# A selective scan beside routed experts: the first quarter of the scan moved into the attention stage, expert rows scatter-added, and a product moved from GpSimd to VectorE

## The chip, the cores and the metric

One core of a Trainium2 chip runs the whole kernel in one launch, in float32. Its engines are TensorE (PE in the rows, with PEld for its weight loads), VectorE (DVE), ScalarE (ACT), GpSimd (POOL) and SyncE (SP), which issues most DMAs. The metric is the device time of one execution in microseconds, and lower is better. Each engine works through its own instructions in order and waits on semaphores that the others raise, so the place of an instruction in its engine's order matters as much as its duration.

## The reference, cut to what matters

`x` is 4 sequences (batches) of 512 tokens with 512 features, `ctx` is 4 x 512 x 256. Four blocks follow one another, each with a residual addition:

```python
x = x + attention(layernorm(x), ctx)      # energy = (ctx Wq + bq)(ctx Wk + bk)^T, softmax, mixes feature rows
x = x + moe16(layernorm(x))               # 16 experts of 192, top 2 per token, weights from a softmax
x = x + mamba(ctx, layernorm(x))          # selective scan over ctx, gated by silu(layernorm(x))
x = x + ffn2(layernorm(x))                # 2 of 8 experts of 2048, chosen once for all tokens

# mamba, for one batch: 512 channels, 16 states per channel, 512 time steps
xin = in_proj(ctx); u = silu(conv4(xin) + conv_b)
dt_low, Bm, Cm = split(x_proj(u)); dt = softplus(dt_proj(dt_low) + dt_b)
state = state * exp(dt * A) + (dt * u) * Bm      # the recurrence over time
y = sum_n(state * Cm) + D * u;  out = y * silu(z)
```

What the scan needs comes from `ctx` alone. Only its gate `z` needs the result of the first two blocks. In moe16 a token's two expert outputs are weighted and added to the token's row `x1`, which gives `x2`.

## The kernel before, in words

The work runs in five stages.

1. **The sequence stage**, a loop over the 4 batches (`sequence_pe`, `sequence_act`, `sequence_dve`, `sequence_transfers`; `rstd_of` on GpSimd). Per batch: queries and keys, four energy tiles (L1460), softmax (`row_max`, `normalize`), transposes (L1437), the mixing products (L1474), the sum with x (L1148), a layernorm, its transposes, the router scores (L1494). Between these lie the scan's inputs: `in_proj` (L1430) for the next batch, the convolution (`convolve`, L1108 and L1114), silu (L856), `x_proj` (L1480), `dt_proj` (L1484), and the softplus of `dt`, whose exp and ln are on ScalarE (L866, L871) and whose five passes over 128x2048 are on VectorE (`softplus`, L1131 to L1140). The step sizes `DT` and `DTU` of all batches stay in SBUF; u, the rows of B and C, x1 and the normalised rows go to DRAM.
2. **The routing stage**: VectorE ranks the tokens by expert and makes one-hot tables `row_hot` and `tile_hot` (L1229 to L1238), and TensorE turns them into the slot list `slot_tok` with 32 products (L1516). There are 48 slot tiles of 128 rows.
3. **The recurrence stage** holds the scan and the 16 experts together. The scan is cut into 128 units, 32 a batch. A unit is one block of 128 channels with two states: ScalarE makes the decay (`decay`, two exps, L892), GpSimd `dt*u*B` (`dbu`, L728), VectorE scans (L1247) and multiplies with C (`read_out`, L1256), TensorE adds the two products to y (`add_states`, L1534); after each four units ScalarE takes y out of its bank (`take_y`). The expert path of a tile is: gather rows of xn by an indirect DMA from GpSimd (`gather`, L742), transpose (L1554), gate and up products (`up`, L1561), a copy to SBUF and tanh on ScalarE, gate times up on GpSimd (`gate_by_up`, L734), `finish_h` on VectorE (L1262), transpose, the down product (`down`, L1579), a scaled copy to `YT` and a plain store of it to `expert_rows`. The interleaving is written out by hand: 8 units ahead, then a fixed share of the remaining ones in each tile:

```python
AHEAD = 8
ALL = B * UB
cuts = [AHEAD + (ALL - AHEAD) * j // SLOT_TILES for j in range(SLOT_TILES + 1)]
...
for j in range(SLOT_TILES):          # VectorE
    for i, u in enumerate(units(j)):
        scan(*bu(u))
        if i == 1 and j + 1 < SLOT_TILES:
            finish_h(0, j + 1)
        read_out(*bu(u))
```

   so a tile has 2.5 units. In a tile TensorE does `turn_h(j)`, `up(j+1)`, some units, `turn_x(j+2)`, more units, `down(j)`.
4. **The combine stage**, per batch: GpSimd gathers each token's two expert rows (`gather_y`, eight indirect DMAs a batch), VectorE adds them with their weights to x1 (`add_first`, `add_second`), takes the statistics, gates y and adds (`combine`); ScalarE and TensorE normalise, transpose and make the logits of the last block (`silu_z`, `turn_gated`, L1000 to L1008). At its end the two experts are known.
5. **The last feed-forward stage**, bound to TensorE by its three-term products (L1664, L1675).

## Time and profile before

| | |
|---|---|
| median of three runs | 1596.02 us (1595.16 to 1596.70) |
| profiled execution, first to last instruction | 1594.7 us |
| its own time beside that span | not reported apart from the three runs; their median is 1.3 us above the span |
| TensorE, matmul busy | 1391.5 us (87%) |
| VectorE busy | 936.9 us (59%) |
| GpSimd busy | 784.0 us (49%) |
| ScalarE busy | 709.8 us (45%) |
| chain that ended last | TensorE 58%, VectorE 22%, issue 10% |

The span has five stages with different limits, so the shares over the whole say little. In the page's 40 slices VectorE is at 9 tenths only in slices 8 to 18, which is the recurrence stage; TensorE is at 9 in the last 18 slices, the last feed-forward. Between them both are partly idle. A row of a stage has to be read against that stage's own length.

### The profile page before, as it was taken

The page shows a single profiled execution, that of the slowest core. Times are in us where ns is not written, and L with a number is a line of the kernel's source. Part 1 is how long each engine was busy: PE and PEld are TensorE (multiplying, and loading weights), DVE is VectorE, ACT ScalarE, POOL GpSimd, SP SyncE. Part 2 cuts the span into 40 slices and gives each one's busy share as a digit, 9 for nine tenths or more (in the row PEclk, how much of TensorE's full clock was granted, in tenths as well). Part 3 has the DMA queues.
Part 4 walks back from the last instruction along what each step waited for, and adds up shares of the span by engine and source line. Part 5 has one row for each costly group of instructions (what it writes and reads, how often), then busy time and mean ns, then how long its engine had stood idle before and what let it go on. Part 6 is the DMA issues. An engine that isn't in the chain of part 4 may idle for free.

```text
span 1594.7 us, 18873 instructions
## 1 busy us (share of the span) xinstructions
PE 1391.5 (87%) x6080; PEld 1030.4 (65%) x6080; DVE 936.9 (59%) x1186; ACT 709.8 (45%) x1303; POOL 784.0 (49%) x607
## 2 busy tenths in 40 slices
PE   6988983588899989897166999999999999999998
PEld 3535532566666656664166787878787887878786
DVE  2677767999999999998683224241414224241413
ACT  4445433266766776665143333333333333333332
POOL 0000000788888988885631445444544545444442
PEclk9898895699999999999555999999999999999999
DMA  3202214477977987863655900010000100010000
GB/s 105 108 26 81 107 53 165 158 240 257 315 257 234 319 269 264 281 198 125 218 198 203 364 14 0 0 66 1 14 0 13 52 13 0 0 53 0 0 0 26
DMA packets 78202, 191.29 MB, mean 120 GB/s; under 512 B 10856, under 2 KB 15752, under 8 KB 77120
## 3 DMA queue, kind: packets, MB, share of 16 engines
q1 hardware_dynamic: 64832, 157.03, 29.3%
q0 software_dynamic: 6400, 20.98, 4.1%
q10 hardware_dynamic: 6912, 12.59, 2.2%
q8 instruction: 28, 0.46, 0.1%
q14 instruction: 30, 0.25, 0.0%
HBM read 152.55 MB, written 38.01 MB: 119 GB/s over the span
## 4 chain that ended last, share of the span: by engine, by line
PE 58%; DVE 22%; issue 10%; ACT 4%; POOL 3%; DMA 3%; ACTq 0%; SPq 0%; DVEq 0%; POOLq 0%
PE decay L1675 22%; PE bank L1664 21%; DVE decay L1247 11%; DVE S L1256 4%; PE bank L1474 2%; PE decay L1430 2%; PE bank L1437 1%; DVE XH L1114 1%; PE bank L1494 1%; PE bank L1534 1%; PE decay L1484 1%; PE bank L1619 1%; POOL Y L767 1%; PE bank L1561 1%; PE decay L1480 1%
## 5 line engine op out<-in xcount | busy, mean ns | idle before, releaser
L1387 DVE CAST HFH<-HF 128x512 fp32r<-128x512 f32 x128 | 59.0, 461 | 496.7 <-ACT HF L1045 496.7
L815 POOL TENSOR_TENSOR W2L<-W2R,W2H 128x512 fp32r<-128x512 f32 x128 | 172.5, 1347 | 348.2 <-ACT W2H L1040 348.2
L728 POOL TENSOR_TENSOR S<-DTU,Bb 128x1024 f32<-128x1024 f32 x128 | 304.7, 2401 | 25.1 <-DVE row_hot L1229 21.7
L1247 DVE TENSOR_TENSOR_SCAN decay<-decay,S 128x1024 f32<-128x1024 f32 x128 | 292.9, 2288 | 0.5 <-ACT decay L892 0.5
L1664 PE MATMUL bank<-XSH,W1H 128*128 128x512 f32 x512 | 202.9, 396 | 4.2 <-POOL W1L L811 4.2
L1675 PE MATMUL decay<-W2H,HFH 128*128 128x512 f32 x512 | 200.4, 391 | 5.3 <-DVE HFL L1389 5.3
L1664 PE MATMUL bank<-XSH,W1L 128*128 128x512 f32 x512 | 203.0, 396 | 0.0
L1664 PE MATMUL bank<-XSL,W1H 128*128 128x512 f32 x512 | 202.3, 395 | 0.0
L1675 PE MATMUL decay<-W2L,HFH 128*128 128x512 f32 x512 | 199.9, 390 | 0.0
L1675 PE MATMUL decay<-W2H,HFL 128*128 128x512 f32 x512 | 199.7, 390 | 0.0
L811 POOL TENSOR_TENSOR W1L<-W1R,W1H 128x512 fp32r<-128x512 f32 x128 | 171.1, 1337 | 49.6 <-ACT W1H L1031 49.6
L1040 ACT CAST W2H<-W2R 128x512 fp32r x128 | 79.4, 620 | 230.0 <-PE decay L1675 229.7
L1045 ACT ACTIVATE HF<-bank,b1T 128x512 f32<-128x512 f32 x128 | 88.3, 690 | 195.4 <-PE bank L1664 195.3
L892 ACT ACTIVATE decay<-DT,negA 128x511 f32<-128x511 f32 x256 | 166.3, 683 | 0.0
L1534 PE MATMUL bank<-ident,S 128*128 128x128 f32 x1024 | 136.9, 284 | 32.3 <-ACT U L933 16.3
L1256 DVE TENSOR_TENSOR S<-decay,Cb 128x1024 f32<-128x1024 f32 x128 | 156.1, 1219 | 4.2
L1534 PEld LDWEIGHTS bank<-ident,S 128*128 128x128 f32 x1024 | 122.8, 148 | 54.5 <-issue 28.3
L1561 PE MATMUL bank<-WGU,XGT 128*128 128x384 f32 x384 | 133.3, 491 | 0.7 <-ACT XGT L900 0.7
L695 POOL TENSOR_TENSOR rstd<-vare,minus_half 128x4 f32<-128x4 f32 x8 | 8.1, 1011 | 227.4 <-DVE vare L1072 227.4
L1675 PEld LDWEIGHTS decay<-W2H,HFH 128*128 128x128 f32 x512 | 96.1, 188 | 30.2 <-issue 8.8
L1664 PEld LDWEIGHTS bank<-XSH,W1H 128*128 128x128 f32 x512 | 96.6, 189 | 27.1 <-POOL W1L L811 5.7
L1664 PEld LDWEIGHTS bank<-XSH,W1L 128*128 128x128 f32 x512 | 96.5, 188 | 23.1
(212 smaller groups left out, 2102.3 us busy)
## 6 DMA issues: line engine op xcount, KB each, us to landing
WGU<-in_L_ffn_gate_w SPq DMA_DIRECT2D x48, 384.0 KB, 3.8
WGU<-in_L_ffn_up_w SPq DMA_DIRECT2D x48, 384.0 KB, 5.1
WD<-in_L_ffn_down_w SPq DMA_DIRECT2D x48, 384.0 KB, 4.9
Bb<-bc_rows SPq DMA_DIRECT2D x32, 512.0 KB, 7.9
Cb<-bc_rows SPq DMA_DIRECT2D x32, 512.0 KB, 9.7
expert_rows<-YT ACTq DMA_DIRECT2D x48, 256.0 KB, 4.2
W1R<-in_L_ffn_w SPq DMA_DIRECT2D x6, 1024.0 KB, 13.9
W2R<-in_L_ffn_w SPq DMA_DIRECT2D x6, 1024.0 KB, 14.1
```

The lines of the kernel that those rows point to most:

```text
L728: pool.tensor_tensor(S[u % NP][:], DTU[:, ds(b, 1), c, :].to_broadcast([P, PAIR, L]), Bb[j][:], ALU.mult).then_inc(dbu_ready, 1)
L811: pool.tensor_tensor(W1L[f % 2][:], W1R[:, ds(e, 1), :, f * P:(f + 1) * P].rearrange("p e k f -> p (e k) f"), W1H[f % 2][:].bitcast(F32), ...
L815: pool.tensor_tensor(W2L[f % 2][:], W2R[:, ds(e, 1), f, :].rearrange("p e d -> p (e d)"), W2H[f % 2][:].bitcast(F32), ALU.subtract).then_i ...
L892: ins = act.activation(DA[u % 2][:, i, 1:], DT[:, ds(b, 1), c, 1:].rearrange("p b l -> p (b l)"), ACT.Exp, scale=negA[:, c, j * PAIR + i:j ...
L1040: act.copy(W2H[f % 2][:], W2R[:, ds(e, 1), f, :].rearrange("p e d -> p (e d)")).then_inc(w2h_ready, 1)
L1045: act.activation(HF[f % 2][:], PS[4 + f % 2][:], ACT.Gelu_apprx_tanh, bias=b1T[:, ds(e, 1), f:f + 1].rearrange("p e f -> p (e f)")).then_i ...
L1247: dve.tensor_tensor_scan(flat, flat, S[u % NP][:].rearrange("p i l -> p (i l)"), 0.0, ALU.mult, ALU.add).then_inc(scan_done, 1)
L1256: dve.tensor_tensor(S[u % NP][:], DA[u % 2][:], Cb[j][:], ALU.mult).then_inc(hc_ready, 1)
L1534: ins = pe.matmul(YS[:, t * P:(t + 1) * P], st[:, i, t * P:(t + 1) * P], ident[:], start=(i0 + i + t == 0), stop=False, is_transpose=True, ...
L1561: ins = pe.matmul(UP[:, 0:2 * F].rearrange("p (g f) -> p g f", g=2), XGT[n % 2][:, k, :], WGU[n % 2][:, :, k, :], start=(k == 0), stop=(k ...
L1664: ins = pe.matmul(PS[4 + f % 2][:], w[f % 2][:, k, :], v[half][:, k, :], start=(k == 0 and i == 0), stop=(k == K - 1 and i == 2))
L1675: ins = pe.matmul(PS[t][:], u_[f % 2][:, t * P:(t + 1) * P], w[f % 2][:], start=(f == 0 and i == 0), stop=(f == FT - 1 and i == 2))
```

## The change

The scan's first batch (32 units) moves into the sequence stage, eight units a round, one round beside the attention of each batch and the projections of the next. The projections and step sizes of batch 0 are now made before the first round. The loops over batches become written-out rounds. 80 units remain for the 48 tiles, eight before them and eight behind them. The PSUM banks 5 to 7 go round in one fixed list of jobs, each waiting until the job three before it has been read. Three of the softplus passes move to GpSimd (`step_sizes`), both layernorm applications to ScalarE (`norm_x`, `norm_x1`). The expert outputs are weighted in the copy to `YT` and added straight into the rows of x1 in DRAM by an indirect DMA with an addition; the gathers and additions of the combine stage go. The slot table carries weights as well as tokens. Gate times up moves from GpSimd to VectorE.

```diff
-        AHEAD = 8
-        cuts = [AHEAD + (ALL - AHEAD) * j // SLOT_TILES for j in range(SLOT_TILES + 1)]
+        EARLY = UB
+        ROUND = EARLY // B
+        AHEAD = EARLY + 2 * HP
+        cuts = [AHEAD + (ALL - AHEAD - TAIL) * j // SLOT_TILES for j in range(SLOT_TILES + 1)] + [ALL]
...
 # GpSimd
+            def step_sizes(b):
+                dt, dtu, rl = DT[:, b], DTU[:, b], XP[:, :, TAPS - 1:]
+                pool.wait_ge(nd_ready, b + 1)
+                pool.tensor_tensor(rl, rl, ZZ[:], ALU.subtract).then_inc(size_made, 1)
+                pool.wait_ge(ln_ready, b + 1)
+                pool.tensor_tensor(dt, rl, dt, ALU.add).then_inc(size_made, 1)
+                pool.tensor_tensor(dtu, dt, dtu, ALU.mult).then_inc(dt_ready, 1)
...
+            for b in range(B):
+                n = b * ROUND
+                products(n + 3, n + ROUND)
+                scale_and_shift1(2 * b + 2)
+                products(n + ROUND, n + ROUND + 2)
+                if b + 1 < B:
+                    scale_and_shift1(2 * b + 3)
+                    step_sizes(b + 1)
+                products(n + ROUND + 2, n + ROUND + 3)
...
+            def add_rows(j):
+                pool.wait_ge(yt_ready, j + 2)
+                if j:
+                    pool.wait_ge(yt_added, j * DMA)
+                pool.indirect_dma_start(out=x2_rows, out_offset=bass.IndirectOffsetOnAxis(ap=slot_dst[:, j:j + 1], axis=0),
+                                        in_=YT[j % 2][:], in_offset=None, compute_op=ALU.add).then_inc(yt_added, DMA)
...
             for j in range(SLOT_TILES):
                 for u in units(j):
                     dbu(*bu(u))
-                gate_by_up(j)
+                if j >= 2:
+                    add_rows(j - 2)
                 if j + 2 < SLOT_TILES:
                     gather(0, j + 2)
...
 # ScalarE, one round
+                exp_e(b, 0); exp_e(b, 1); decays(n + 1, n + 2)
+                take_turned("v", b, 0, XNT); take_turned("v", b, 1, XNT)
+                exp_e(b, 2); exp_e(b, 3); decays(n + 2, n + 3)
...
+                silu_u(b + 1); decays(n + 6, n + 7)
+                take_qk(b + 1); take_xd(b + 1); decays(n + 7, n + 8)
+                norm_x1(b); size_abs(b + 1)
+                for t in range(T): take_turned("n", b, t, XNT)
+                size_exp(b + 1); take_scores(b); size_ln(b + 1); norm_x(b + 1)
+                decays(n + 8, n + 9)
...
 # VectorE, one round
+                row_max(b, 0); row_max(b, 1); unit(n)
+                normalize(b, 0); row_max(b, 2); normalize(b, 1); row_max(b, 3); unit(n + 1)
+                normalize(b, 2); normalize(b, 3); unit(n + 2)
+                convolve(b + 1, (0, 1)); unit(n + 3); unit(n + 4); convolve(b + 1, (2, 3)); unit(n + 5)
+                add_x(b, 0); add_x(b, 1); unit(n + 6); add_x(b, 2); add_x(b, 3); statistics_x1(b); unit(n + 7)
+                positive_part(b + 1); statistics_x(b + 1); correction(b + 1)
...
 # VectorE, routing and tiles
+                for t in range(NT):
+                    dve.tensor_scalar(tile_hot[:, k, t, 0, :], iota_j[:], jf[:, k, t:t + 1], tokid[:, t:t + 1], ALU.is_equal, ALU.mult)
+                    ins = dve.tensor_scalar(tile_hot[:, k, t, 1, :], iota_j[:], jf[:, k, t:t + 1], rwt[:, k, t:t + 1], ALU.is_equal, ALU.mult)
...
+                    last = i == len(units(j)) - 1 and j + 1 < SLOT_TILES
+                    if last:
+                        gate_by_up(j + 1)
                     scan(*bu(u))
-                    if i == 1 and j + 1 < SLOT_TILES:
+                    if last:
                         finish_h(0, j + 1)
                     read_out(*bu(u))
...
 # TensorE, one round (the last without the steps of b + 1)
+                energy(b, 0); energy(b, 1); turn_xn(b, 0); turn_xn(b, 1); sums(n - 1, n)
+                energy(b, 2); energy(b, 3); sums(n, n + 1); turn_xn(b, 2); turn_xn(b, 3)
+                turn_ctx(b + 1); in_proj(b + 1, (0, 1)); sums(n + 1, n + 2); in_proj(b + 1, (2, 3))
+                turn_p(b, 0); turn_p(b, 1); sums(n + 2, n + 3); turn_p(b, 2); turn_p(b, 3); sums(n + 3, n + 4)
+                mix(b, 0); mix(b, 1); sums(n + 4, n + 5); mix(b, 2); mix(b, 3); sums(n + 5, n + 6)
+                queries_keys(b + 1); x_proj(b + 1); sums(n + 6, n + 7); dt_proj(b + 1)
+                turn_xn1(b, t) for the four t; score(b)
...
 # VectorE, combine: add_first and add_second are gone
+            for u in units(SLOT_TILES):
+                scan(*bu(u))
+                read_out(*bu(u))
+            statistics_x2(0)
+            statistics_x2(1)
```

The diff is cut: calls that stand on lines of their own in the code are put together here.

## Rows read from the trace of the kernel before

**Rows 1.** Windows by stage: length, busy of PE PEld DVE ACT POOL, clock, DMA, GB/s.

```profile
0.00:262.20 262.20, 214.94 (x696) 115.00 (x696) 164.69 (x285) 118.03 (x174) 10.84 (x19) 0.88 0.22 77
262.20:294.50 32.30, 2.04 (x4) 1.17 (x4) 29.07 (x101) 2.81 (x7) 10.40 (x8) 0.50 0.80 292
294.50:752.30 457.80, 407.36 (x2038) 285.92 (x2038) 447.28 (x306) 298.94 (x665) 379.68 (x271) 0.96 0.74 242
752.30:862.20 109.90, 55.04 (x268) 51.35 (x268) 71.42 (x161) 35.80 (x55) 44.50 (x54) 0.57 0.59 201
862.20:1594.70 732.50, 712.13 (x3074) 576.97 (x3074) 224.49 (x339) 254.18 (x402) 338.59 (x256) 0.99 0.11 40
```

**Rows 2.** Timeline of the sequence stage: start us, us, engine line operation.

```profile
21.30 7.13 PE L1430 MATMUL decay<-ctxT,inT 128*128 128x512 f32 x16 [0.40 <-ACT gate2T L823]
...
34.39 0.69 DVE L1088 TENSOR_REDUCE nmax<-bank 128x1 f32<-128x512 f32 x1 [7.99 <-PE bank L1460]
```

**Rows 3.** Windows, one batch of the sequence stage, from one first row maximum to the next.

```profile
34.39:93.01 58.62, 53.29 (x161) 27.60 (x160) 41.30 (x71) 26.94 (x39) 2.02 (x2) 0.85 0.20 73
```

**Rows 4.** Groups by line and shape in one batch: busy us, mean ns, idle before.

```profile
L1474 PE MATMUL bank<-ATT,XNT 128*128 128x512 f32 x32 | 14.3, 599 | 1.4 <-DVE X1A L1148 0.7 <-ACT ATT L838 0.7
L1114 DVE SCALAR_TENSOR_TENSOR XH<-XP,convW,XH 128x512 f32<-128x512 f32 x12 | 8.2, 747 | 0.1
L1133 DVE SCALAR_TENSOR_TENSOR ND<-XH,ZZ 128x2048 f32<-128x2048 f32 x1 | 2.3, 2293 | 0.0
```

**Rows 5.** Timeline around the end of the sequence stage.

```profile
255.24 1.91 ACT L871 ACTIVATE ZZ<-XH 128x2048 f32<-128x2048 f32 x1 [2.22 <-DVE ND L1133]
...
262.17 1.31 DVE L1172 MAX8 M<-SC 128x8 f32<-128x16 f32 x16
```

**Rows 6.** Windows, the router scores of two batches, at two granted clocks.

```profile
129.50:136.50 7.00, 7.00 (x33) 7.00 (x34) 4.04 (x12) 5.45 (x6) 1.01 (x1) 0.50 0.01 3
246.10:250.20 4.10, 4.08 (x32) 3.98 (x32) 0.00 (x0) 4.07 (x6) 0.00 (x0) 0.90 0.00 0
```

**Rows 7.** Timeline: the slot tables, and a small tensor_scalar of the combine stage.

```profile
284.63 3.96 DVE L1233 TENSOR_TENSOR tile_hot<-iota_j,jf 128x768 f32<-128x768 f32 x2
...
288.63 5.99 DVE L1238 TENSOR_TENSOR tile_hot<-tile_hot,tokid 128x768 f32<-128x768 f32 x2
...
294.67 13.89 PE L1516 MATMUL bank<-tile_hot,row_hot 128*128 128x48 f32 x64 [24.91 <-DVE tile_hot L1238]
...
861.07 0.36 DVE L1362 TENSOR_SCALAR loh<-iota_e,lidf 128x8 f32<-128x8 f32 x2
```

**Rows 8.** Groups by shape in 300 us of the recurrence stage (400 to 700).

```profile
L728 POOL TENSOR_TENSOR S<-DTU,Bb 128x1024 f32<-128x1024 f32 x85 | 200.6, 2380 | 0.8
L1247 DVE TENSOR_TENSOR_SCAN decay<-decay,S 128x1024 f32<-128x1024 f32 x85 | 194.5, 2289 | 0.5 <-ACT decay L892 0.5
L1256 DVE TENSOR_TENSOR S<-decay,Cb 128x1024 f32<-128x1024 f32 x85 | 103.6, 1219 | 2.6
L1534 PE MATMUL bank<-ident,S 128*128 128x128 f32 x680 | 90.0, 282 | 19.3 <-ACT U L933 11.8 <-ACT DTU L935 7.4
L1554 PE MATMUL bank<-ident,XG 128*128 128x128 f32 x135 | 23.5, 296 | 10.3 <-DMA XG<-xn_rows,gcol 5.6 <-ACT HT L910 4.6
L1262 DVE SCALAR_TENSOR_TENSOR GU<-bank,GU 128x192 f32<-128x192 f32 x34 | 11.6, 342 | 2.0 <-POOL GU L734 2.0
```

**Rows 9.** DMA issues of the recurrence stage: count, size, median us to landing.

```profile
expert_rows<-YT ACTq DMA_DIRECT2D x48, 256.0 KB, 4.2
...
XG<-xn_rows,gcol POOLq DMA_INDIRECT x48, 6.2
```

**Rows 10.** Timeline of the combine stage.

```profile
764.77 2.74 DVE L1299 SCALAR_TENSOR_TENSOR X<-Y,rwt,X 128x512 f32<-128x512 f32 x4 [12.44 <-DMA Y<-expert_rows,pcol]
...
846.92 2.93 ACT L1000 ACTIVATE ZN<-X,shift,rstd 128x512 f32<-128x512 f32 x4
...
858.90 0.19 ACT L1008 COPY logits<-bank 128x32 f32<-128x32 f32 x1 [2.63 <-PE bank L1619]
```

1076 lines of the change are left out of this document (623 added, 453 removed).

## The prediction

> **What bounds the kernel now.** I read the windows by stage first, because the limits differ [rows 1]. The sequence stage (0 to 262.2) has TensorE busy 82%, VectorE 63%, GpSimd 4%. The recurrence stage (294.5 to 752.3) has VectorE busy 447.3 of 457.8 us: it is the limit there, and TensorE with 407.4 us (89%) is close behind. The combine stage (109.9 us) has no engine over 65%. The last stage, 732.5 us, is TensorE's and isn't touched: I leave it as it is. So the reader is to see a full VectorE in one stage, room on VectorE in another, and a TensorE that is nearly full in both. Moving scan units helps by what VectorE gets rid of until TensorE binds; where they go, they cost what the tighter order of the rounds makes of them.
>
> I sum against the profiled span, 1594.7 us. The median of the three runs is 1.3 us above it and I add that at the end.
>
> **Sequence stage, the period of a round.** Now a batch takes 58.6 us, with TensorE busy 53.3 and VectorE 41.3 [rows 3]. In the new round VectorE loses two layernorm applications and three passes of 2.3 us [rows 4] (some 11 us) and gains eight units. A unit is 2.29 + 1.22 = 3.5 us [rows 8], so 28 us: about 58 to 60 us of work. TensorE gains eight times 90.0/85 = 1.06 us, the additions of U (1.6) and the transposes of ctx (2): about 65 us as this row counts it. Neither sum is the period, for the orders of the engines chain. I followed one round from the first scan (time 0), with durations of 0.7 for a 128x512 operation on VectorE, 0.55 for a copy and 1.4 for a decay on ScalarE, 3.6 for one mixing product (14.3/4, rows 4) and 3.6 for x_proj or a pair of in_proj ([rows 2]: four channels in 7.1):
> - three units with the softmax between them end at 14.6; the first half of the convolution (8.2/2 for its additions plus 1) waits for two in_proj copies at 15.2 and ends at 20; two units, 27; the second half, 32; sixth unit, 35.7;
> - x_add needs two mixing products, done in time; seventh unit 40.5; x_add and statistics 45;
> - the eighth unit waits for its decay, which stands on ScalarE behind `take_xd`: TensorE can begin x_proj only at 45.3, since the third mixing bank is freed at 41 and the keys come first. x_proj 48.9, copy 49.5, decay 50.9, unit 54.4: a stall of 5.9 us;
> - positive part 57.4 with the fourth dt product waiting for a bank; the four transposed copies of the normalised x1 end at 60.3; exp 62.3; correction (1.2 + 2.3) 65.9;
> - scores on TensorE until 65 to 68, and ScalarE takes them before its ln: ln, a table load of 1.3, four normalisations 2.9, a decay 1.4. The next first scan comes at 75 to 78.
>
> So a round is 76.5 us. Its last third holds some 10 us in which VectorE has only two row maxima. GpSimd's three passes of 128x2048 (estimate 2 x 2.38 = 4.8 each [rows 8]) end 4.6 us after the first scan, and its third unit product at 7.1 is due at 11.1: hidden; on less cover (a round 4 us shorter there) they would be the wait.
>
> First scan of round 0: in_proj starts at about 21.9 instead of 21.3 [rows 2], convolution in halves to 36, silu, x_proj, dt_proj and positive part to 47.7, exp and correction 54.5, ln and three passes on VectorE (7) 61.4, first product and decay 64. Three periods: 293.5. The last round has no next batch: units and additions to 35.9, statistics, normalisation, transposes, scores to 51: 344.5. Before, the routing began at 262.2 [rows 5]. **+82.3 us.**
>
> At this point the clock matters. The same 32 score products take 7.0 us at a granted clock of 0.50 and 4.1 at 0.90 [rows 6], so the level of 1.2 GHz costs up to 3 us in each round in which TensorE has waited before; the range 75 to 78 holds it. The Trainium skill (TensorE: Matmul & The Clock Gate, What's actually happening) says that idleness brings the half clock and activity releases it; the rounds add idle gaps on TensorE, and by that rule every round would pay the 7 and not the 4, which is the 78 end: three rounds at 78 give +4.5 us, no other outcome.
>
> **Routing.** `tile_hot` was four operations, 3.96 + 5.99 = 9.95 us [rows 7], and is 64 tensor_scalars of 128x48. No row has these; a 128x8 one with a scalar operand has a pitch of 0.18 (0.36 for two). I take 0.20: 12.8 us, **+2.9**; ends 0.08 (the pitch of the 128x16 maxima, 1.31/16, rows 5) and 0.25 give -4.8 and +6. The slot products get 96 columns instead of 48: 64 in 13.9 us at clock 0.50, 0.217 each [rows 7]; with 16 columns they also take 0.217 (7.0/32 [rows 6]), so columns are nearly free: +1, at most 8. Five small operations on the slot sums, 1.2 us. **+2.2.** `spare_row` and the removed `pos` cast: nothing.
>
> **Recurrence stage.** Eight units before the tiles and eight behind are VectorE's, 28 us each. Between them 48 tiles of 1.67 units instead of 2.5. VectorE needs 1.67 x 3.5 = 5.8 plus gate times up (0.35, as its neighbour of the same 192 columns) and finish: 6.3 us. TensorE: 407.4 minus the slot products 13.9 minus 128 x 1.06 leaves 257.8, or 5.37 a tile; with 1.67 units 7.14, of which about 0.2 falls with the additions of U: 6.95. To this its waits: 19.3 us in 85 units for y being taken (0.38 a tile) and 10.3 in 34 tiles for gathered rows (0.30) [rows 8]. That is 7.6 us: **TensorE binds instead of VectorE.** The loop through the copy of gate and up, the product on VectorE, a whole scan, finish, transpose and the next up product is 0.5 + 0.35 + 2.3 + 0.35 + 0.2 + 2.75, 6.5 us, just under it: the product before the last scan stalls VectorE, but not the tile. GpSimd: 1.67 x 2.38 and two indirect DMAs at about 1.3: 6.6, covered. So 28 + 48 x 7.6 + 28 = 420.8 against 457.8: **-37.0 us.**
>
> The new wait is in `add_rows`: the DMA of tile j-2 waits until that of j-3 has landed, and behind it on GpSimd stand the gather of tile j+2 and the unit products; for them wait TensorE's transposes and VectorE's scan. No row shows an adding DMA. A plain store lands in 4.2 us, an indirect gather in 6.2 [rows 9]. I take 7, near the gather; 4.2 is the low end, and twice the gather, 12.4, the high one. Up to 7.6 it costs nothing. The rule in the Trainium skill (DMA: Bandwidth & Descriptors, Two DMAs through the same engine are not ordered) speaks against shortening this: dependent DMAs need the first one's completion, so the chain can't overlap, and the tile can't be shorter than the landing. No run here shows it yet; it is the third rival below.
>
> DMA traffic: the stage moved 242 GB/s at a share of 0.74 [rows 1], so 327 at full share. The tiles carry 48 x 1.7 MB (weights 1.18, rows in and out 0.52) and 20 MB of B, C and u, 102 MB in 365 us, 280 GB/s, 0.86: it fits; if an addition takes its bytes twice, 0.96, and the margin is gone.
>
> **Combine.** Before: VectorE idles 12.4 us for the first gathers [rows 10], and the stage is 109.9 us. Now the loads of x2 run under the last eight units. Statistics 3.2, power and shift 1.4, silu 2.9, last transposes 0.9: 8.6 us; gate, add, statistics, shift 9.7: first normalisation at 18.3. Per batch then 12.0 from normalisation to logits (846.92 to 858.90 [rows 10]) and 2.9 for the next silu before it: 18.3 + 4 x 12.0 + 2 x 2.9 + 0.5 = 72.6, plus 3.3 to the end of the stage: 76. Half the TensorE work at a higher clock would give 66. **-33.9 us.**
>
> **Sum:** 82.3 + 2.9 + 2.2 - 37.0 - 33.9 = +16.5. 1594.7 + 16.5 + 1.3 = **1612.5 us**.
>
> **Rivals.**
> - *The tiles run at TensorE's bare work* (the waits for y and for rows vanish since ScalarE and DMA have more room a tile): 6.95 us, -31 us, **1581**, faster. For it: the engine that caused the order of waits, VectorE, is off the path. Against: those waits came with ScalarE 65% busy in the stage [rows 1], not with a full one. It decides from a tile under 7.19 us (16.5 + 3.2 over 48).
> - *The rounds overlap better than my chain*: with banks and decays in time a round is TensorE's 66 us: -31.5, **1581**. For it: TensorE is the fuller engine. Against: `decays` stand behind `take_xd` and behind the ln in the order.
> - *The adding DMA lands late*: at 9.5 us a tile is 9.5: +91, **1704**; at 8.5 +43, **1656**. Decides from 7.6 us. For it: the read before the write; against: a load of 0.86 is not full.
> - *The change's parts cancel*: either faster case by half, **1596**.
>
> **Numbers.** Forecast with its own spread (1600 to 1630) 0.52; bare tiles 0.15; overlapping rounds 0.11; late additions 0.14; cancelling 0.08. What can be told from no change here is 0.2%, 3.2 us. Faster 0.15 + 0.11 = 0.26; same 0.08; slower 0.66. The range that leaves 2 in 10 out reaches over both faster cases' middle and the mild form of the late one: 1576 to 1650.
>
> **What would show it.** Right: the first slot-table maximum near 345 and first rows of maxima 76 us apart; in the tiles TensorE over 90% and VectorE about 83%; from the last read-out to the last expert choice 76 us. Wrong: a period near 66, a tile under 7.2 us, or a wait of GpSimd on the landing of the added rows in most tiles. The last stage longer or shorter than 732 us would mean that something I left alone was touched.

## The result and the profile after

The kernel after took 1721.0 us (median of four runs, 1707.05 to 1722.28) against 1595.6 of the kernel before: a ratio of 1.077, 95% interval 1.073 to 1.081. The forecast was 1612.5 in a range of 1576 to 1650: the sign was right, the size was not, and the range did not hold it. The profiled execution of the kernel after spans 1720.5 us, the one of before 1594.7, so the stages below add up to the whole difference. Where the runs of one kernel spread by more than 1.5% (x2 and x11 below), only those within that of the quickest are compared.

Windows of the kernel after by stage: length, busy time of PE PEld DVE ACT POOL, granted clock, DMA share, GB/s. They answer to [rows 1]; the recurrence is cut here into the units ahead of the tiles, the tiles, and the units behind them.

```profile
0.00:391.70 391.70, 282.51 (x968) 163.26 (x969) 274.88 (x316) 189.18 (x312) 129.78 (x68) 0.77 0.24 81
391.70:443.50 51.80, 4.38 (x15) 2.35 (x13) 49.68 (x161) 3.40 (x8) 19.11 (x12) 0.53 0.30 119
443.50:472.40 28.90, 21.03 (x116) 18.04 (x116) 28.28 (x22) 11.49 (x25) 10.24 (x7) 0.71 0.40 137
472.40:885.60 413.20, 351.14 (x1582) 228.77 (x1583) 311.60 (x259) 231.49 (x510) 308.39 (x173) 0.94 0.84 238
885.60:915.20 29.60, 15.61 (x62) 11.03 (x60) 24.17 (x16) 10.55 (x23) 12.64 (x6) 0.58 0.46 151
915.20:988.70 73.50, 54.65 (x268) 50.51 (x268) 49.87 (x129) 35.49 (x55) 10.24 (x16) 0.57 0.35 129
988.70:1720.50 731.80, 711.73 (x3074) 576.80 (x3074) 224.35 (x338) 254.17 (x402) 338.51 (x256) 0.99 0.11 40
```

| stage, us | before | after | difference | forecast |
|---|---|---|---|---|
| sequence | 262.2 | 391.7 | +129.5 | +82.3 |
| routing | 32.3 | 51.8 | +19.5 | +2.9 |
| recurrence | 457.8 | 471.7 | +13.9 | -34.8 (with the slot sums) |
| combine | 109.9 | 73.5 | -36.4 | -33.9 |
| last feed-forward | 732.5 | 731.8 | -0.7 | 0 |

So three terms failed and two held. Of the 109 us between forecast and time, 47 are in the sequence stage, 17 in the routing and 49 in the recurrence stage; the combine stage takes 2.5 back.

The forecast's own signs agree with this. The first slot-table maximum comes at 391.7 instead of near 345. In the tiles TensorE is busy 85% and VectorE 75% (351.14 and 311.60 of 413.20 us), where over 90% and about 83% were named for the right case. The sign of the late addition, a wait of GpSimd on the landing of the added rows in most tiles, did not come either: it waits so in 10 of the 48, 34.4 us in all.

**Routing.** The timeline of the kernel after, at the slot tables (start, duration, engine, line, operation). All 64 tensor_scalars have one shape; while GpSimd's eight unit products run (413.14 to 431.56), each takes 2.33 to 2.38, and from the moment these end, 0.29 at a pitch of 0.215.

```profile
412.97 0.30 DVE L1447 TENSOR_SCALAR CbT<-iota_j,jf,tokid 128x48 f32<-128x48 f32 x1
413.19 2.33 DVE L1449 TENSOR_SCALAR CbT<-iota_j,jf,rwt 128x48 f32<-128x48 f32 x1
415.44 2.38 DVE L1447 TENSOR_SCALAR CbT<-iota_j,jf,tokid 128x48 f32<-128x48 f32 x1
...
429.22 2.38 DVE L1447 TENSOR_SCALAR CbT<-iota_j,jf,tokid 128x48 f32<-128x48 f32 x1
431.52 0.29 DVE L1449 TENSOR_SCALAR CbT<-iota_j,jf,rwt 128x48 f32<-128x48 f32 x1
431.73 0.29 DVE L1447 TENSOR_SCALAR CbT<-iota_j,jf,tokid 128x48 f32<-128x48 f32 x1
...
413.14 18.42 POOL L774 TENSOR_TENSOR S<-DTU,Bb 128x1024 f32<-128x1024 f32 x8 [20.71 <-DVE row_hot L1442]
```

**Rounds.** Two rounds of the kernel after, from first scan to first scan. The third takes 88.0. Forecast: 76.5, with TensorE busy 65, and busy it is for 65.5 and 67.7.

```profile
70.09:156.80 86.71, 65.46 (x228) 36.62 (x228) 67.27 (x78) 46.13 (x77) 30.87 (x15) 0.80 0.16 56
156.80:246.25 89.45, 67.65 (x240) 39.12 (x240) 70.51 (x78) 46.10 (x77) 34.91 (x16) 0.79 0.29 101
```

VectorE's groups by shape in the second of them: busy us, mean ns | idle before. In [rows 4] the same shapes took 747 ns (convolution) and 2293 (correction).

```profile
L1322 DVE TENSOR_TENSOR_SCAN decay<-decay,S 128x1024 f32<-128x1024 f32 x8 | 18.3, 2293 | 11.0 <-ACT decay L996 11.0
L1275 DVE SCALAR_TENSOR_TENSOR DTU<-XP,convW,DTU 128x512 f32<-128x512 f32 x12 | 12.6, 1093 | 0.2
L1331 DVE TENSOR_TENSOR S<-decay,Cb 128x1024 f32<-128x1024 f32 x8 | 9.8, 1224 | 0.3
L1264 DVE TENSOR_SCALAR X1A<-X1A,rinv 128x512 f32<-128x512 f32 x4 | 4.8, 1212 | 0.1
L1297 DVE SCALAR_TENSOR_TENSOR ZZ<-DT,ZZ 128x2048 f32<-128x2048 f32 x1 | 4.3, 4318 | 0.0
L1289 DVE TENSOR_SCALAR XP<-bank,dtB 128x512 f32<-128x512 f32 x4 | 2.8, 744 | 1.6 <-PE bank L1658 1.6
```

The reader is to see which rows grew. The scan, the read-out and the positive part have an operand in PSUM (`decay`, `bank`) and kept their durations; the convolution, the normalisation and the correction have all their operands in SBUF and grew. Among those that read one tensor from SBUF, the statistics (BATCH_NORM_STATS2, 0.68 us) did not. The convolution grows in all three rounds (1.09 us each); the correction only in this one, and takes 2.29 us in the other two. The waits for ScalarE's decay (11.0) were in the forecast's chain in part: 5.9 for the eighth unit, and the rest as the wait for the next first decay.

**Tiles.** The starts of ScalarE's copy of gate and up, one a tile, give 47 tile lengths. The median is 7.7 us; the forecast had 7.6 for each. But six tiles take 12.2 to 14.7, 83 us together, and the mean is 8.4. The timeline of the tile that takes 14.7:

```profile
584.57 0.99 POOL L827 DMA_INDIRECT XG<-xn_rows,slot_tok  x1 [0.31 <-issue]
...
588.51 0.47 ACT L1099 COPY GU<-bank 128x384 f32<-128x384 f32 x1
...
592.98 1.60 POOL L836 DMA_INDIRECT x_rows<-YT,slot_dst  x1 [5.02 <-DMA x_rows<-YT,slot_dst]
594.31 1.12 PE L1789 MATMUL bank<-ident,XG 128*128 128x128 f32 x4 [5.15 <-DMA XG<-xn_rows,slot_tok]
594.88 0.99 POOL L827 DMA_INDIRECT XG<-xn_rows,slot_tok  x1 [0.30 <-issue]
...
603.19 0.48 ACT L1099 COPY GU<-bank 128x384 f32<-128x384 f32 x1 [1.63 <-PE bank L1796]
603.70 0.43 DVE L1457 TENSOR_TENSOR GU<-GU 128x192 f32<-128x192 f32 x1 [10.08 <-ACT GU L1099]
```

GpSimd waits 5 us for the landing of the last addition, and the next gather and the unit products stand behind it. But the rows for which TensorE waits 5 us are not those: they are of the gather issued at 584.57, before that wait, and it was itself 9.7 us on the way. VectorE then stands 10 us in front of the gate product, behind which its scans stand.

Five of the six long tiles begin like this one: in the tile before them an addition and, 1.9 us behind it, a gather are issued, and both take 8.3 to 10.8 us to land. In these stretches the DMA engines are full. SyncE has put loads of B and C (512 KB each) and of u beside the weights of the experts there. Windows over two of the five, from the issue of the late addition to the landing of the gather, and over the sixth tile (DMA share and GB/s are the last two numbers):

```profile
582.70:594.30 11.60, 6.08 (x26) 3.43 (x25) 10.88 (x10) 6.11 (x14) 6.26 (x4) 0.95 1.04 302
764.50:777.20 12.70, 6.14 (x26) 3.82 (x26) 9.06 (x9) 5.94 (x13) 7.63 (x6) 0.88 1.05 303
852.60:866.90 14.30, 9.35 (x38) 5.84 (x36) 12.85 (x6) 3.68 (x9) 7.91 (x5) 0.76 0.24 49
```

Of the 96 gathers and additions of this kernel, 41 share no moment with a load of B, C or u; they land after 5.9 us in the median and 7.5 at most. 43 share one with two or more such loads, and their median is 7.7; all 20 that take over 8 us are among them. The sixth long tile has nothing of this. It holds one of the two gate products that GpSimd shut out in these tiles (the other, 4.26 us long, comes right behind it):

```profile
853.15 5.83 DVE L1457 TENSOR_TENSOR GU<-GU 128x192 f32<-128x192 f32 x1 [3.65 <-ACT GU L1099]
```

### The profile page after: what moved, and what is told of

It is laid out like the page before. It is cut to its first block, busy times and chain, and to the rows that moved or that the text cites. A ratio compares the mean times of both kernels' runs of the same rounds, so it can differ in the third digit from the quotient of the medians.

```text
span 1720.5 us, 18682 instructions
## 1 busy us (share of the span) xinstructions
PE 1441.0 (84%) x6080; PEld 1050.8 (61%) x6080; DVE 962.8 (56%) x1234; ACT 735.8 (43%) x1334; POOL 828.9 (48%) x536
## 3 DMA queue, kind: packets, MB, share of 16 engines
q0 software_dynamic: 10752, 25.17, 6.8%
## 4 chain that ended last, share of the span: by engine, by line
PE 49%; DMA 8%; DVE 8%; issue 5%; POOL 4%; ACT 3%; SPq 0%; ACTq 0%; DVEq 0%; POOLq 0%
PE decay L1916 20%; PE bank L1905 20%; DMA XG<-xn_rows,slot_tok 5%; PE bank L1796 2%; DMA x_rows<-YT,slot_dst 2%; DVE decay L1322 2%; PE bank L1814 2%; PE bank L1702 2%; POOL S L774 2%; POOL x_rows L836 2%; DVE S L1331 1%; DVE CbT L1447 1%; PE bank L1860 1%; DVE CbT L1449 1%; ACT decay L996 1%
## 5 line engine op out<-in xcount | busy, mean ns | idle before, releaser
L1702 PE MATMUL bank<-ident,S 128*128 128x128 f32 x1024 | 152.4, 300 | 44.8 <-DVE S L1331 38.9
L1702 PEld LDWEIGHTS bank<-ident,S 128*128 128x128 f32 x1024 | 133.7, 156 | 78.9 <-DVE S L1331 45.2
L836 POOL DMA_INDIRECT x_rows<-YT,slot_dst x48 | 76.8, 1599 | 87.4 <-ACT YT L1112 50.4
L1331 DVE TENSOR_TENSOR S<-decay,Cb 128x1024 f32<-128x1024 f32 x92 | 112.2, 1219 | 3.2
## 6 DMA issues: line engine op xcount, KB each, us to landing
W1R<-in_L_ffn_w SPq DMA_DIRECT2D x6, 1024.0 KB, 13.9
W2R<-in_L_ffn_w SPq DMA_DIRECT2D x6, 1024.0 KB, 14.7
```

The source lines that it names most:

```text
L836: pool.indirect_dma_start(out=x2_rows, out_offset=bass.IndirectOffsetOnAxis(ap=slot_dst[:, j:j + 1], axis=0), in_=YT[j % 2][:], in_offset= ...
L1331: dve.tensor_tensor(state(b, u)[:], DA[u % 2][:], Cb[rows(b, j)][:], ALU.mult).then_inc(hc_ready, 1)
L1702: ins = pe.matmul(YS[:, t * P:(t + 1) * P], st[:, i, t * P:(t + 1) * P], ident[:], start=(i0 + i + t == 0), stop=False, is_transpose=True, ...
```

## The experiments

Two theories were tested against the rivals "slow by themselves", "hidden anyway" and "the DMA engines are full". (A) VectorE and GpSimd shut each other out when both read SBUF. (B) The order of gather, addition and gate product in GpSimd's and VectorE's queues makes the long tiles. Stage lengths of all kernels, each of its profiled execution. The tiles go here from the first scan of the first tile to the first scan behind the last one, 403.5 us in the kernel after (the 413.2 of the windows above begins some 6 us earlier and ends 3.5 later); combine ends with the choice of the two experts.

| kernel | sequence | routing | 8 ahead | tiles | behind | combine |
|---|---|---|---|---|---|---|
| before | 262.2 | 32.3 | 28.4 | 429.4 | none | 108.4 |
| after | 391.7 | 51.8 | 35.1 | 403.5 | 33.1 | 71.9 |
| x1 products behind `tile_hot` | 389.2 | 38.6 | 35.9 | 399.8 | 33.2 | 71.8 |
| x2 gather first | 390.6 | 52.8 | 34.8 | 566.0 | 32.3 | 71.5 |
| x3 no addition | 385.0 | 51.8 | 34.5 | 389.4 | 31.9 | 71.3 |
| x4 none early, gate on GpSimd | 310.1 | 38.6 | 32.8 | 448.4 | 32.3 | 71.2 |
| x5 two targets | 390.3 | 37.7 | 35.7 | 385.2 | 31.9 | 71.2 |
| x6 decays earlier | 383.2 | 37.7 | 36.1 | 401.8 | 31.9 | 71.2 |
| x7 sizes on VectorE | 386.5 | 37.6 | 36.2 | 398.2 | 32.2 | 71.5 |
| x8 gate on GpSimd | 388.5 | 38.6 | 32.9 | 420.8 | 32.0 | 71.7 |
| x9 short products | 357.5 | 38.6 | 35.7 | 399.5 | 33.3 | 71.7 |
| x10 sixteen early | 358.5 | 38.6 | 31.0 | 421.4 | 31.5 | 71.3 |
| x11 none early, gate on VectorE | 314.6 | 38.6 | 32.8 | 522.3 | 30.4 | 71.2 |
| x12 before, products behind `tile_hot` | 258.6 | 28.8 | 33.0 | 429.2 | none | 108.7 |
| x13 gather first, gate on GpSimd | 388.6 | 52.7 | 30.7 | 391.2 | 33.0 | 72.0 |
| x14 rounds mended | 382.7 | 37.7 | 36.4 | 393.9 | 32.5 | 71.5 |
| x15 before, four behind | 262.7 | 32.4 | 28.4 | 412.8 | 14.5 | 101.4 |
| x16 before, eight behind | 262.6 | 32.4 | 28.4 | 415.5 | 30.6 | 101.0 |
| x17 x15 and x12 | 260.8 | 28.7 | 32.9 | 420.2 | 15.9 | 100.6 |
| x18 after, all mended | 382.9 | 37.7 | 31.6 | 397.1 | 31.4 | 71.2 |

Each row is one execution, so small differences in it mean nothing. Six kernels have the same code in the sequence stage (after, x1, x2, x3, x8, x13), and it takes 385.0 to 391.7 us there; six have the same code in the tiles (after, x1, x6, x7, x9, x14), which take 393.9 to 403.5.

### The shut-out in the routing

```diff
-            pool.wait_ge(hot_ready, 1)      # x1; x12 the same on the kernel before, with 1 + TOP
+            pool.wait_ge(hot_ready, 2)
```

> GpSimd makes the eight products ahead of the tiles only when tile_hot is complete (it waited for row_hot alone). Theory: VectorE and GpSimd shut each other out of a shared path to the memory, so the eight 128x48 tensor_scalars that take 2.33 to 2.38 us each while GpSimd's products run fall to about 0.29 with a pitch of 0.215; tile_hot takes 64 x 0.215 = 13.8 us instead of 30.4, the first scan behind it waits 2.4 for its product, so the stage of the routing is 51.8 - 16.6 + 2.6 = 38 us and the kernel 1707. Rival: the first eight are slow by themselves (the start of a run of such instructions, or CbT's place); then they stay at 2.3 and the kernel is 1721 + 2.4 = 1723.

1705.7 us, ratio to before 1.068 (1.064 to 1.073). The routing fell from 51.8 to 38.6, as the theory had it: all 64 operations now take 0.30. The rival falls.

> The kernel before (1595.4 us), with GpSimd's first products behind tile_hot instead of behind row_hot. Theory of the shared path: its four operations on tile_hot, which took 9.95 us while a product ran, take about 0.9 each (768 columns at the 1.08 ns a column of the 4096 of row_hot), 3.5 in all, and the first scan then waits 2.4 for its product: 1591. Rival: they take 10 us by themselves, and the wait adds 2.4: 1598.

The kernel before had the same shut-out, and [rows 7] shows it. The timeline of x12:

```profile
281.10 1.82 DVE L1233 TENSOR_TENSOR tile_hot<-iota_j,jf 128x768 f32<-128x768 f32 x2
282.95 1.83 DVE L1238 TENSOR_TENSOR tile_hot<-tile_hot,tokid 128x768 f32<-128x768 f32 x2
...
287.37 2.30 DVE L1247 TENSOR_TENSOR_SCAN decay<-decay,S 128x1024 f32<-128x1024 f32 x1 [2.59 <-POOL S L728]
```

3.65 us instead of 9.95, and 2.59 given back in the wait for the first product; the units ahead take 4.6 longer. The kernel is not told from unchanged (ratio 0.9998, 0.9987 to 1.0009): the theory's durations are right and its 1591 us is not.

### The shut-out in the rounds

```diff
+                w = slice(0, L // 8 if n < EARLY else L)
-                pool.tensor_tensor(state(b, u)[:], DTU[:, b:b + 1, c, :]..., Bb[rows(b, j)][:], ALU.mult)
+                pool.tensor_tensor(state(b, u)[:, :, w], DTU[:, b:b + 1, c, w]..., Bb[rows(b, j)][:, :, w], ALU.mult)
```

> On the kernel in which the products wait for tile_hot (1705.7 us, sequence 389.2, rounds of 87.5, 86.6 and 88.9). GpSimd's products of the 32 units in the rounds cover only the first 64 of the 512 columns (left out: the rest of the rows of batch 0, which keep a zero; four more memsets at the start). All waits and all work of the other engines stay. Theory: the products shut VectorE out: its normalisations go from 0.74 to 1.3 us back to 0.49, the additions of the convolution from 1.09 to 0.75, the correction from 4.3 to 2.3, together 9 to 10 us a round; 7 of them shorten the round: sequence 365, kernel 1682. Rival: VectorE's longer operations only fill time in which it would wait for TensorE and ScalarE; the round stays within 1.5 us: 1701 to 1710.

1678.4 us, against 1705.7 for the kernel that it changes; sequence -31.7 (forecast of the theory: -24). The rounds are 78.3, 77.7 and 78.4 us. VectorE's groups in the second round of x9:

```profile
L1278 DVE SCALAR_TENSOR_TENSOR DTU<-XP,convW,DTU 128x512 f32<-128x512 f32 x12 | 8.6, 755 | 0.2
L1292 DVE TENSOR_SCALAR XP<-bank,dtB 128x512 f32<-128x512 f32 x4 | 2.8, 746 | 1.6 <-PE bank L1661 1.6
L1300 DVE SCALAR_TENSOR_TENSOR ZZ<-DT,ZZ 128x2048 f32<-128x2048 f32 x1 | 2.4, 2426 | 0.0
```

Against x1 the rounds are 9.2, 8.9 and 10.5 us shorter, 9.5 in the mean, and VectorE is busy 9.2, 9.8 and 6.9 us less in them. With the shut-out by unit products gone the round is within 2 us of the 76.5 of the forecast. VectorE waits for decays 10.2 us in this round, against 11.0 in the kernel after, so that wait isn't the difference. Nor is it that the shorter products come earlier: in the rounds of x1 no scan waits for a product.

```diff
-                    step_sizes(b + 1)                 # GpSimd, x7
+                    first_step_sizes(b + 1)           # VectorE, behind correction(b + 1): the same three passes
```

> On the kernel in which the products wait for tile_hot (1705.7 us). The three passes of 128x2048 that make the step sizes of batches 1 to 3 are VectorE's again (2.3 us each, 6.9 a round, behind the correction) and not GpSimd's (4.2 to 4.6 each, 13 a round). Theory: GpSimd's passes shut VectorE out for about as long as VectorE would need for them (normalisations 1.29 us instead of 0.49, additions of the convolution 1.0 instead of 0.75): VectorE's others become short again and the round changes by -2 to +2 us: kernel 1700 to 1712. Rival: GpSimd's passes were hidden and free, the round becomes 5 to 7 us longer three times: 1721 to 1727.

1697.9 us, ratio 1.065 (1.062 to 1.069), not told from x1's 1.068 (1.064 to 1.073). VectorE works 7.7, 8.0 and 5.4 us more in a round and the round stays (88.8, 88.4, 86.3 beside 87.5, 86.6, 88.9). The result is that of the theory, but only a part of its reason holds: the convolution stays at 1.09 us, so it was the unit products that made it long, while the four normalisations of the second and third round fall to 0.49 us each, from 0.74 and 1.13. Most of the passes fits into time in which VectorE stood: its idle time in a round fell from 19.8, 18.0 and 21.7 to 13.4, 11.8 and 13.7 us.

```diff
-                take_qk(b + 1); take_xd(b + 1); decays(n + 7, n + 8)
+                decays(n + 7, n + 8); take_qk(b + 1); take_xd(b + 1)
...
-                size_exp(b + 1); take_scores(b); size_ln(b + 1); norm_x(b + 1); decays(n + 8, n + 9)
+                size_exp(b + 1); decays(n + 8, n + 9); take_scores(b); size_ln(b + 1); norm_x(b + 1)
```

> On the kernel in which the products wait for tile_hot (1705.7 us, sequence 389.2). On ScalarE the decay of the eighth unit of a round stands ahead of the copies of queries, keys and x_proj, and the decay of the next round's first unit ahead of the scores, the ln and the normalisation. Theory: the two stalls of VectorE in each round (5.9 and 5 to 5.9 us) come from that order; the first goes, of the second half stays since the products need the step sizes: three rounds each 5 us shorter, sequence 374, kernel 1691. Rival: what VectorE waits for next (the fourth dt product, the energies of the next batch) ends no earlier; sequence within 4 us of 389, kernel 1702 to 1710.

1699.9 us, ratio 1.067 (1.063 to 1.070), by itself not told from x1. The sequence is 6.0 shorter in the profiled execution, between the theory's 15 and the rival's 4, and it is 382.7 to 383.2 in all three kernels with this edit (x6, x14, x18), below the 385.0 to 391.7 of those without. The waits for decays are gone from the rounds, and the three together are 11.0 us shorter (81.1, 85.3, 85.6); the last round, 60.3 instead of 55.3, gives 5 back.

### The price of the sequence stage's new order

```diff
-        EARLY = UB
+        EARLY = 0         # x4; with x1's wait and gate_by_up on GpSimd behind the unit products (x11: on VectorE)
```

> No scan unit stands in the sequence stage (all 128 behind the routing, eight ahead of the tiles and eight behind), GpSimd makes the product of gate and up as in the kernel before, and the products wait for tile_hot as in the first run of this call; the adding of rows, the new routing and the new combine stage stay. Theory: the loss is in the rounds, and what the tiles had to gain by fewer units was not there. Sequence 262 to 275, routing 36, recurrence 28 + 48 x 8.4 (2.33 units of 3.5 and 0.2 as in the kernel before) + 28 = 459, combine 73.5, last stage 731.8: 1568, faster than both kernels. Rival 1: the adding DMA holds a tile at 8.6 whatever VectorE does: recurrence 469, 1578. Rival 2: the sequence stage is slow by its new order of banks and copies, not by the units: sequence 300 or more, 1600 or more.

1674.7 us, not 1568, and slower than before by 5%. Rival 2 came: the sequence stage takes 310.1 with no unit in it. The timeline of x4 at its first row maxima, for [rows 2]:

```profile
66.52 0.68 DVE L1241 TENSOR_REDUCE nmax<-bank 128x1 f32<-128x512 f32 x1
...
125.77 0.68 DVE L1241 TENSOR_REDUCE nmax<-bank 128x1 f32<-128x512 f32 x1
...
191.49 0.68 DVE L1241 TENSOR_REDUCE nmax<-bank 128x1 f32<-128x512 f32 x1
```

The first softmax starts at 66.5 instead of 34.4, since the whole input path of batch 0 stands before it: +32.1. The periods are 59.3, 65.7 and then 68.0 instead of 58.6, and the last batch gets a little back: the other 15.8. The units come on top: 389.2 - 310.1 = 79 us for 32.

But about half of the miss of 107 us is in the recurrence stage, 513.5 us where the theory had 459. A version of the kernel before can be set beside it: x16 (below) has the same 8 units ahead, 112 in the tiles and 8 behind, the gate product on GpSimd too, and stores the expert rows. Windows over the tiles of x4 and then of x16:

```profile
381.50:829.90 448.40, 380.36 (x1852) 260.20 (x1850) 393.73 (x272) 278.69 (x613) 409.88 (x252) 0.96 0.84 239
323.40:738.90 415.50, 375.65 (x1854) 259.32 (x1854) 394.46 (x272) 275.13 (x614) 351.07 (x253) 0.97 0.79 258
```

TensorE and VectorE do the same work, GpSimd 59 us more (it issues the additions), and the tiles take 33 us more. The combine stage is 30 shorter (71.2 and 101.0). So the adding path pays in the tiles about what it saves in the combine stage. The two kernels differ in the tiles in small things as well (the place of `finish_h`, the order of the loads), so the 33 us are not shown to be the additions' alone.

```diff
-        EARLY = UB
+        EARLY = 16        # x10: four units a round, tile_hot in the place of three states
```

> Sixteen units in the sequence stage, four a round, instead of 32 (1705.7 us) or none (1674.7); 2.0 units to a tile; the gate product on VectorE, tile_hot in the place of three states. Theory: a unit costs 2.5 us in a round (389.2 - 310.1 over 32), so sequence 350; a tile of 2.0 units has 7.7 us of VectorE and 8 of TensorE and takes 8.5: tiles 408; routing 38, ahead and behind 68, combine 71, last stage 734: 1669 and 3 more: 1672. Rival: TensorE, whose units are moved and not removed, holds the tile at what 1.58 units take (8.3): tiles 400, 1664. Other rival: the late rows of the gathers grow with the density of the stage: tiles 424, 1688.

1690.1 us, near the third guess. Sixteen units cost 48 us in the sequence stage, the next sixteen 31. What the tiles gain by them depends on the engine of the gate product. With it on GpSimd, 32 early units shorten the tiles from 448 (x4) to 421 (x8), for 79 us in the rounds. With it on VectorE the tiles go from 522 (x11, below) to 421 (x10) to 400 (x1): the first sixteen units pay there, the next sixteen don't. None of these kernels is faster than the 1674.7 us with no early unit and the gate product on GpSimd.

### Gather, addition and gate product in the tiles

```diff
-                if j >= 2: add_rows(j - 2)
-                if j + 2 < SLOT_TILES: gather(0, j + 2)
+                if j + 2 < SLOT_TILES: gather(0, j + 2)
+                if j >= 2: add_rows(j - 2)
```

> In GpSimd's order of a tile the gather of tile j+2 stands ahead of the addition of tile j-2 instead of behind it. Theory: the gather is late because it waits in line behind the addition (its 1.6 us of issue, and its wait for yt_ready and for the last landing); TensorE's 40.5 us of waits for gathered rows mostly go, half of it is given back to the next wait: tile stage 413.2 - 20 = 393, kernel 1700. Rival: the rows are late because the DMA engines are full (share 0.84), whatever the order of issue: the waits move, stage within 4 us of 413, kernel 1717 to 1725.

1816.8 us in the one run of four that can be compared: slower by 96 where I had expected 20 faster. The others took 1852.5 to 1884.1, and the profiled execution is the longest of them, so its rows show what happens and not how much of it happens in 1816.8 us. Groups of x2 in its tiles:

```profile
L1457 DVE TENSOR_TENSOR GU<-GU 128x192 f32<-128x192 f32 x47 | 191.2, 4068 | 97.3 <-ACT GU L1099 97.3
L836 POOL DMA_INDIRECT x_rows<-YT,slot_dst x47 | 75.0, 1595 | 253.9 <-ACT YT L1112 253.9
```

The gate product, 0.35 us of work on two operands in SBUF, took 4.07 on average (0.58 in the kernel after): 46 of the 48 met a unit product of GpSimd, 31 of them two in a row, and stood until these were through. It makes a ring: the gate product late, the down product late, YT late, so GpSimd waits 5.4 us for YT and starts its unit products just when the next gate product is due. The next runs test this.

```diff
                 for u in units(j): dbu(*bu(u))
+                gate_by_up(j)                         # GpSimd, x8; gone from VectorE
```

> On the kernel in which the products wait for tile_hot (1705.7 us, tiles 399.8). The product of gate and up of a tile is GpSimd's again, behind the unit products. Theory: VectorE, which stands 94 us in the stage before this product while ScalarE's copy of gate and up isn't there, scans ahead instead; GpSimd has 3.8 + 1.6 + 1.0 + 0.6 = 7.0 us a tile and stays under 8.3: tiles 399.8 - 12 = 388, kernel 1694. Rival: the product comes later behind GpSimd's wait for the landing of the added rows, and the up and down products with it: tiles 410, kernel 1716.

1719.1 us (x1: 1705.7); tiles +21. With the old order the rival was right: the gate product stands behind GpSimd's waits, and VectorE waits some 120 us for it in the tiles.

x11 is x4 with the gate product left on VectorE, x13 the kernel after with the edits of x2 and x8.

> No unit in the sequence stage, as in the run of 1674.7 us, but the product of gate and up is VectorE's. Theory: GpSimd was full in the tiles there (2.33 products of 2.44, 1.6 to issue the addition, 1.0 for the gather, 0.6 for the gate product: 8.9 us with its waits): without the gate product it has 8.3 and VectorE 2.33 x 3.5 + 0.7 = 8.9: tiles 448.4 - 18 = 430, kernel 1657. Rival: VectorE is the limit at 8.9 and stands for ScalarE's copy beside it: tiles 448 or more, 1675.

1746.0 us (median of three runs, ratio 1.095, 1.089 to 1.101): tiles 522 where the theory had 430. Gate products of up to 7.9 us, mean 1.96; 20 of the 48 take over 1 us, against 2 in the kernel after. Why they meet so often at 2.33 units a tile is not shown; in x10, with 2.0, it is 1 of 48.

> The kernel after (1721 us) with the gather ahead of the addition, which made its tiles 566 us long, but with the product of gate and up on GpSimd. Theory: those tiles were long because VectorE's gate product was shut out for the length of GpSimd's two unit products in nearly every tile (mean 4.15 us for 0.35 of work), and TensorE, ScalarE and the addition waited for it in a ring; with the product in GpSimd's own order there is nothing to shut out and the tiles take what they take with the gate product on GpSimd and the old order, 421 (405 to 435): kernel 1740. Rival: the gather ahead of the addition delays the additions themselves; tiles stay above 500, kernel over 1815.

1703.4 us, ratio 1.065 (1.062 to 1.068) where the kernel after had 1.077 (1.073 to 1.081); tiles 391.2. The order that cost 96 us or more with the gate product on VectorE costs nothing with it on GpSimd: the two edits together gain 17.6 us, of which 4.4 are in the units ahead. So the loss of x2 came with VectorE's gate product, and the ring is shown. The tiles' own 12 us are not clear of their spread (393.9 to 403.5 with the old order; this order has 391.2 here and 397.1 in x18). The 30 us against x8, where only the place of the gather differs in the tiles, are. Groups of x13:

```profile
L841 POOL DMA_INDIRECT x_rows<-YT,slot_dst x47 | 75.0, 1596 | 44.0 <-DMA x_rows<-YT,slot_dst 28.3 <-issue 10.5 <-ACT YT L1118 3.9
L826 POOL TENSOR_TENSOR GU<-GU 128x192 f32<-128x192 f32 x47 | 51.2, 1090 | 3.5 <-ACT GU L1105 3.5
```

```diff
-                if j: pool.wait_ge(yt_added, j * DMA)
-                pool.indirect_dma_start(out=x2_rows, ...
+                if j >= 2: pool.wait_ge(yt_added[j % 2], j // 2 * DMA)
+                pool.indirect_dma_start(out=(x2_rows, x2_odd)[j % 2], ...      # x5
```

> On the kernel in which the products wait for tile_hot (1705.7 us, tiles 399.8 us). Even tiles add their rows to x2, odd tiles to a second tensor with a semaphore of its own, so an addition waits for the landing of the one two tiles before and not for the last one (left out: the second tensor isn't read, so x2 lacks the odd tiles' rows; five more stores of 1 MB in all stand in the sequence stage). Theory: the chain of landings holds the tiles (35% of the chain of waits of that kernel between 500 and 800 is the landing of added rows, pieces of 8 to 9.7 us): the 47 us of waits for it go, and part of the 41 us for gathered rows behind it: tiles 399.8 - 30 = 370, kernel 1676. Rival: the DMA engines are the limit; the additions then land later in pairs and the stage stays within 8 us: 1698 to 1714.

1694.5 us, ratio 1.065 (1.060 to 1.070), not told from x1 by time alone; tiles -14.6, half of the theory and outside the rival's 8, and 8.7 below the shortest with the single chain. The chain of landings is worth some 10 to 15 us. Five tiles of 10.6 to 13.4 us are left: the rival is right in part, for the rows that come late beside the loads of B, C and u still come late.

```diff
-                in_=YT[j % 2][:], in_offset=None, compute_op=ALU.add).then_inc(yt_added, DMA)
+                in_=YT[j % 2][:], in_offset=None).then_inc(yt_added, DMA)      # x3
```

> The indirect DMAs that write the experts' rows write them without adding (left out: the addition; the row of x2 is overwritten). Theory: an adding DMA costs more than a writing one in three places, issue on GpSimd (1.6 us against 1.0 of a gather), landing (6.4 us against 4.2 of the plain store of before) and engine time (queue share 24.4% against 8.7%): the DMA share of the tile stage falls from 0.84 to about 0.77, a tile from 8.61 to 8.2 us, kernel 1721 - 20 = 1701. Rival: the addition is hidden, the tiles wait in the loop of copy, product, scan and finish: issue and landing fall but the stage stays at 413 within 4, kernel 1717 to 1725.

1702.1 us (after: 1721.0), ratio 1.068 (1.064 to 1.072); tiles -14.1, 4.5 below the shortest of those that add. Another 6.7 us of the difference are in the sequence stage, which this edit doesn't touch. The issue on GpSimd falls from 1.60 to 1.03 us, the landing from 6.4 to 5.3. The page's row for GpSimd's queue, after and then x3:

```profile
q0 software_dynamic: 10752, 25.17, 6.8%
```

```profile
q0 software_dynamic: 7680, 25.17, 4.0%
```

### Adding up, and versions of the kernel before

x14 has the edits of x1, x6 and x7 together, x18 those of x2 and x8 as well, x17 those of x12 and x15.

> The kernel after with three changes at once: products behind tile_hot, the two decays of a round earlier, and the step sizes on VectorE. Theory: they act in different places (routing -13; decays -6 in the sequence; step sizes in VectorE's stall, -3): 1721 - 22 = 1699 to 1693. Rival: the step sizes on VectorE filled the very stall that the earlier decay takes away; then the two don't add and the rounds get back 5 us each: 1705 to 1712.

1692.1 us, ratio 1.060 (1.057 to 1.062). The sequence is 382.7, as with the decays alone (383.2), so the step sizes on VectorE add nothing to them, as they would if both fill one stall. The routing adds in full, the tiles happened to be 6 us shorter.

> The kernel after with everything that helped: products behind tile_hot, earlier decays, step sizes on VectorE (together 1692.1 us, tiles 393.9 there), and the gather ahead of the addition with the gate product on GpSimd (tiles 391.2 instead of 403.5 where that was done alone). Theory: the two sets add up, tiles 388 to 392, sequence 383, routing 38: 1683 to 1690, which leaves the sequence stage 120 us and the tiles' 390 as the cost of this change. Rival: the gate product on GpSimd costs in the tiles what it cost with the old order (+21): 1710.

1677.3 us (1673.9 to 1688.1), ratio 1.050 (1.048 to 1.052), better than the theory's 1683. The gate product on GpSimd no longer costs: against x14 this pair of edits gains 14.8 us, as it gained 17.6 in x13. But the tiles of the profiled execution (397.1 in a span of 1686.3) are no shorter than in x14, so how much of it is theirs stays open (the units ahead are 4.8 shorter). The kernel stays 82 us above before, and the sequence stage alone is 121 longer.

```diff
+        TAIL = 4          # x15; 8 in x16; DVE, ACT, PE and POOL run units(SLOT_TILES) behind the last tile
+        cuts = [AHEAD + (ALL - AHEAD - TAIL) * j // SLOT_TILES for j in range(SLOT_TILES + 1)] + [ALL]
```

> The kernel before (1595.4 us) with four of its 120 units moved from the tiles to behind the last tile, as in the change, and nothing else of it. Theory: VectorE has the same work in all, the tiles take 48 x 8.66 = 415.7 and the four units 14, together the 429.4 of before, and the first gathers of expert rows lie under the four units: the combine stage loses VectorE's 12.4 us of idle time: 1583. Rival: the tiles don't shrink with the units (each goes by its transfers and TensorE's loop, as the kernel after has it): +14 - 12, 1597.

1592.0 us against 1597.1 of before, ratio 0.9970 (0.9955 to 0.9985): 0.3% faster, between the theory's 1583 and the rival's 1597, and the one version with a median clearly below that of before, by little. Tiles and units behind took 427.3 together (before: 429.4), and VectorE's wait for the first gathers fell from the 12.44 of [rows 10]:

```profile
752.09 2.74 DVE L1308 SCALAR_TENSOR_TENSOR X<-Y,rwt,X 128x512 f32<-128x512 f32 x4 [1.27 <-DMA Y<-expert_rows,pcol]
```

The profile gains 8.8 us, the timed runs 5.

> As the run before it, with eight units behind the last tile (2.33 to a tile). Theory: tiles 48 x 8.37 = 402 and 28 behind, again 430, gathers hidden with room to spare: 1583. Rival: TensorE's 5.37 + 2.33 x 1.06 + 0.7 = 8.5 and its waits hold a tile at 8.7: 418 + 28, +16 - 12: 1599.

1601.5 us, ratio 1.0016 (1.0001 to 1.0032): the rival. Its median is 9.5 us above that of x15, where four more units behind the tiles cost 14 to 16. In the profiles the tiles took 415.5 with 2.33 units and 412.8 with 2.42; but the profiled execution is the longest of the twelve here and among the shortest in x15, so the tiles probably do get somewhat shorter, and by less than the units cost behind them.

> The kernel before with four units behind the last tile (1592.0 us beside 1597.1 of before) and, in addition, GpSimd's first products behind tile_hot (routing 28.8 instead of 32.3 us in the run that did this alone, 1595.0 beside 1595.8). Theory: both act in different places and add up: ratio to before 0.997 - 0.001 to 0.002, 1590 to 1591 us beside 1597. Rival: the later first products are missing ahead of the tiles (GpSimd starts the tiles with fewer states made) and the tiles give the routing's gain back: ratio 0.997 to 0.999.

Ratio 0.9995 (0.9978 to 1.0012), not told from no change. The two don't add up, as the rival had it. The routing gains 3.7 and the units ahead lose 4.5, as in x12; the tiles took 420.2 instead of 412.8 in this one execution.

## Why the prediction was wrong, step by step

- **The round, 76.5 us: the step that failed first.** Its order of events was right (two waits for decays, TensorE not the limit), the durations were not. I took "durations of 0.7 for a 128x512 operation on VectorE" and the correction at "1.2 + 2.3" from a stage in which GpSimd was busy 4%, and moved them beside unit products of 2.4 us on GpSimd. Beside those products VectorE was busy 7 to 10 us more in a round. x9 shows it: with short products the same round takes 78. Three rounds at +11.6 are 35 of the 47 us; the first scan at 70.1 instead of 64 is 6, and the last round (57.4 instead of 51) another 6.
- **The start.** The 30 us for batch 0's input path before the first softmax were in the sum; x4 gives them a price, 32.1. With its periods, which with no unit are already up to 68.0 us instead of 58.6, 47.9 of the stage's 129.5 us have nothing to do with units.
- **Routing, +2.9: the second step that failed, measured +19.5.** The pitch of 0.20 was right (0.215). The cost of an operation beside a GpSimd product was missing: eight of the 64 ran so and cost 2.3 each. The sign was to be read: `tile_hot` took 9.95 for four operations of 768 columns [rows 7], while the operation ahead of it in the same timeline of before, with GpSimd idle, did 4096 columns in 4.42, 1.08 ns each:

```profile
280.29 4.42 DVE L1229 TENSOR_TENSOR row_hot<-iota_r,rf 128x4096 f32<-128x4096 f32 x1
```

  By that pitch the four operations, 3072 columns, cost 3.3, and x12 measured 3.65. I read the 9.95 as the cost of the work that goes and didn't ask why it was so dear.
- **Recurrence, -37.0: wrong, +13.9 with the slot sums.** "TensorE binds instead of VectorE" at 7.6 us a tile is right in size for the median (7.7); with TensorE busy 85% of the stage it doesn't bind in the mean. The mean is 8.4, by six tiles of 12 to 15. This is near the third rival, "the adding DMA lands late", but not in its form: no late landing in every tile, but additions and gathers that take 8 to 11 us now and then. "Up to 7.6 it costs nothing" was held against one value, 7 (the median is 6.4), and a median doesn't price a chain of waits. The traffic was held against an average too, "0.86: it fits", and "a load of 0.86 is not full" was the argument against the rival; in the stretches before five of the six long tiles the share is 0.97 to 1.05. x5 puts some 10 to 15 us on the chain of landings, x3 about as much on the addition. The path as a whole was not priced: x4 has tiles 33 us longer than x16 with it, where the forecast had for it only a second issue on GpSimd. The units ahead and behind took 68 instead of 56 us: 5.0 us of wait for the first copy of gate and up, 5.2 for decays, and the slot sums.
- **The loop, 6.5 us, "just under it".** In it the gate product had 0.35 us. In x2 and x11 it has 4.07 and 1.96. The forecast didn't see that the change put it on an engine where it can be shut out; in the kernel after this happened twice in 48 tiles (mean 0.58).
- **Combine, -33.9: right** (-36.4). **Last stage: right.** Two slips of the sum are small: 3.2, 1.4, 2.9 and 0.9 are 8.4 and not 8.6, and the range that was to hold the mild late case, 1656, ends at 1650.
- **The clock** was granted at 0.79 to 0.80 in the rounds, against 0.85 to 0.88 in the batches of before. TensorE was busy 75% of a round and 90% of a batch, so the expected direction came. With short products and 78 us a round it was 0.83. TensorE's busy time in a round fell by 2 to 5 us then (from 65.6, 68.3 and 69.5 to 63.6, 64.1 and 64.7), which may be a part of the 9.5.

The Trainium skill (SBUF — State Buffer, Who interferes with whom) says that VectorE shares a pair of SBUF ports with GpSimd, and that this is an exclusive lock. A VectorE instruction with two SBUF inputs contends with a GpSimd instruction that reads SBUF; a tensor_scalar or copy in a two-port mode contends as well, and there the one that comes second "fully blocks" for the other's whole instruction; with at most one SBUF input and outside those modes nothing contends. This case's traces agree: 2.38 us for 0.30 of work beside a product of 2.3, and an unchanged 1.22 for the read-out, whose second input is in PSUM. Had I weighed that page instead of the one on DMA order, the rounds and the routing would have come out some 42 us longer (3 x 9.5 and 13.2, by x9 and x1).

What stays open: whether the loads of B, C and u make the gathers and additions late. They stand beside every one of the kernel after that took over 8 us, but no run moves them. A kernel with these loads spread evenly over the tiles would tell, and it wasn't tried.

## What to carry to other kernels

Before moving work beside another engine's, split its operations by where their operands lie: what has two inputs in SBUF on VectorE, or is a tensor_scalar from SBUF to SBUF, is not to be priced from a stage in which GpSimd was idle, and a small product in a loop is the dearest one to expose. A row that costs more than its columns is a symptom to explain before it goes into a sum. Price a queue with a wait in it by the long landings, not by the median, for whatever stands behind that wait inherits them. And hold the DMA share against the busiest few microseconds, not against the stage: 0.84 over the tiles was 1.0 in the stretches that made them long.

## What the runs showed of the hardware

- A 128x48 tensor_scalar with two pointer operands takes 0.30 us at a pitch of 0.215; beside a GpSimd product 2.38.
- A gate product of 128x192 on VectorE takes 0.35 us alone and 4.07 on average (up to 6.2) in x2. In 31 of its 46 long cases it stood through two GpSimd products in a row and did not get in between them, where in the routing one tensor_scalar ended with each product.
- An indirect DMA of 128 rows of 2 KB with an addition keeps GpSimd for 1.60 us, 1.03 without, 0.99 for a gather; it lands after 6.4 us in the median (5.3 without) and moves the same bytes in 10752 packets of the queue instead of 7680.
- In the tiles of the kernel after, gathers and additions land after 5.9 us in the median with no load of B, C or u under way and after 7.7 with two or more; all 20 over 8 us have two or more beside them, and the DMA share there is 0.97 to 1.05.
